# Picked keys stored in threes, and two heads' scores together: one Trainium2 core

## The reference

```python
# L0 attention, d = 4 heads of h = 64
scores = jnp.einsum('bdsh,bdth->bdst', q, k) / SCALE
weights = jax.nn.softmax(scores, axis=-1)
feats = jnp.einsum('bdst,bdth->bdsh', weights, v)
...
# L1 attention: 32 heads of 2, B = 4, S = 512
h = jnp.einsum('bsd,fd->bsf', xn, W1)
pair = jax.nn.relu(h[:, :, None, :] - h[:, None, :, :] + b1)
pair = jax.nn.relu(jnp.einsum('bijf,gf->bijg', pair, W2) + b2)
sim = jnp.einsum('bijg,og->bijo', pair, W3)[..., 0] + b3[0]
sim = sim.at[:, diag, diag].set(0.0)
k_sparse = max(1, int(S * SPARSITY))          # 51
_, top_idx = jax.lax.top_k(sim, k_sparse)
...
scores = jnp.einsum('bhid,bhjd->bhij', q, k) / math.sqrt(HEAD_DIM)
attn = jax.nn.softmax(scores + mask[:, None, :, :], axis=-1)
ao = jnp.einsum('bhij,bhjd->bhid', attn, v)
```

## Time and profile before

| what | us |
|---|---|
| three runs, median (lowest to highest) | 2091.67 (2086.42 to 2092.28) |
| the profiled execution, and its span | 2091.8, 2090.0 |
| PE, DVE, ACT, POOL busy in the span | 1664.5, 1452.1, 1260.5, 1253.6 |
| `first_attention`, first to last scores | 31.4 to 207.1 |
| `pairwise_attention`, first L1217 to end of last L1274 | 677.9 to 2028.0 |

### The profile page before, as it was taken

One profiled execution on the slowest core, in us unless ns is written; L12 is line 12 of the kernel. 1 busy time (PEld: TensorE's weight loads), 2 busy tenths in 40 slices (PEclk: granted clock), 3 DMA queues, 4 the chain that ended last, 5 costly groups with the idle time before them and its releaser, 6 DMA issues. The chain is left out here.

```text
span 2090.0 us, 34828 instructions
## 1 busy us (share of the span) xinstructions
PE 1664.5 (80%) x13143; PEld 680.4 (33%) x13143; DVE 1452.1 (69%) x2776; ACT 1260.5 (60%) x1755; POOL 1253.6 (60%) x1107
## 2 busy tenths in 40 slices
PE   6999687888205999999989889889889889984016
PEld 3444454666104333332222223223223223221014
DVE  4555542333347566998988988889989889986656
ACT  3555301332002999999879779779879779873001
POOL 0000067665562037888888888878877887887721
PEclk9999889999657999999999999999999999997556
DMA  8300133999430001111111111111111111111101
GB/s 281 126 1 1 32 102 125 323 353 324 135 90 21 1 22 50 42 43 44 41 45 42 43 45 42 44 45 44 43 44 45 44 44 44 43 43 49 46 18 41
DMA packets 98263, 157.35 MB, mean 75 GB/s; under 512 B 23088, under 2 KB 66224, under 8 KB 98096
## 3 DMA queue, kind: packets, MB, share of 16 engines
q0 software_dynamic: 40448, 95.49, 15.7%
q1 hardware_dynamic: 40240, 42.85, 6.1%
q10 hardware_dynamic: 17408, 16.78, 2.4%
HBM read 109.94 MB, written 45.09 MB: 74 GB/s over the span
## 5 line engine op out<-in xcount | busy, mean ns | idle before, releaser
L1208 POOL DMA_INDIRECT sgot<-kv_rows,sat x816 | 993.1, 1217 | 350.1 <-issue 245.1
L1376 PE MATMUL spre<-sunit,w2t 128*32 128x512 f32 x8192 | 958.3, 604 | 94.3 <-DVE sunit L1217 89.0
L1335 ACT ACTIVATE sunit<-spre,b 128x1024 f32<-128x1024 f32 x512 | 570.5, 1114 | 170.3 <-PE spre L1376 168.5
L1217 DVE TENSOR_SCALAR sunit<-hneg,hplus 128x512 f32<-128x512 f32 x1280 | 543.6, 487 | 56.2 <-PE spre L1376 53.5
L1329 ACT ACTIVATE sunit<-hneg,hplus 128x512 f32<-128x512 f32 x768 | 521.4, 713 | 0.6 <-PEq L1015 0.6
L1376 PEld LDWEIGHTS spre<-sunit,w2t 128*32 128x32 f32 x8192 | 284.5, 111 | 715.7 <-issue 513.4
L1386 PE MATMUL ssims<-sunit,bands 128*32 128x512 f32 x2048 | 274.3, 603 | 0.4 <-ACT sunit L1335 0.4
L1243 DVE TENSOR_TENSOR sgot<-sgot,q 128x3264 f32<-128x3264 f32 x16 | 56.9, 3558 | 175.7 <-DMA sgot<-kv_rows,sat 175.7
L587 POOL MEMSET ebefore<- 128x128 f32 x1 | 0.2, 205 | 223.0 <-POOLq L221 223.0
L1386 PEld LDWEIGHTS ssims<-sunit,bands 128*32 128x32 f32 x2048 | 73.1, 113 | 156.0 <-issue 153.5
L807 ACT ACTIVATE epxt<-ebank 128x512 f32<-128x512 f32 x64 | 38.2, 597 | 114.4 <-DVE eyout L776 94.2
(11 more groups left out here) (238 smaller groups left out, 1724.4 us busy)
## 6 DMA issues: line engine op xcount, KB each, us to landing
slot_rows<-blank SPq DMA_DIRECT2D x4, 4096.0 KB, 26.7
ewgu<-gate_up SPq DMA_DIRECT2D x128, 128.0 KB, 4.5
exin<-slot_rows POOLq DMA_DIRECT2D x64, 256.0 KB, 5.9
slot_out<-eyout ACTq DMA_DIRECT2D x64, 256.0 KB, 5.2
sgot<-kv_rows,sat POOLq DMA_INDIRECT x816, 2.8
x<-L_attn_x SPq DMA_DIRECT2D x4, 512.0 KB, 5.8
out<-ftmp SPq DMA_DIRECT2D x4, 512.0 KB, 3.2
slot_rows<-erows,eslot POOLq DMA_INDIRECT x64, 2.4
```

Of the source, the lines that this page charges most:

```text
L1208: pool.indirect_dma_start(out=got[:, n % 2, key, :], out_offset=None, in_=k.kv_rows[:, :], in_offset=bass.IndirectOffsetOnAxis(ap=at[:, n ...
L1217: ve.tensor_scalar(out, a, c, 0.0, ALU.add, ALU.max).then_inc(on_vector, 1)
L1335: act.activation(unit2[:, t % 2, 2 * h:2 * h + 2, :], pre[:, h, :, :], ACT.Relu, bias=b2[:, 0:1]).then_inc(hidden, 1)
L1376: mm = pe.matmul(pre[32 * g:32 * g + 32, h, c % 2, :], k.w2t[:, 32 * (g % 2):32 * (g % 2) + 32], unit1[:, t % R, 2 * c + g // 2, :], start ...
```

## The change

In `pairwise_attention` the products of a tile go to a new tensor `prod` of shape [17, 64, 3]: 51 keys are 17 groups of three, and the three keys of a group lie next to each other for each of 64 (dimension, head). `weigh_keys` reads `got` in order and writes `prod`, in steps of three numbers (12 bytes); `add_dims`, `take_peak_off` and the exp go through it in order; the reductions read runs of three; `weigh_values` reads `got`, and the weights in steps of three, and writes `prod` in steps of three, in two halves by dimension, the second of which writes over the weights. `add_dims` is two instructions too. `score` and one half of `sim` are gone, and `peak`, `total`, `inv`, `mixed` move into `blank` (all in SBUF). The search rounds stand at steps 2, 3, 5, 9, 10, 11 and 15, the pieces of the attention at steps without a round where there is one (4, 6, 7, 8, 13, 14, and 0, 1, 2 of the next tile), each between first-layer instructions. The exp is at step 9. In every fourth step one of ACT's three first-layer rows goes to VectorE.

In `first_attention` the units of a pair of heads alternate between the two heads, and in each even slot PE makes the scores of two units, from the two halves of the partitions.

```diff
+        def unit(u):
+            pair, within = divmod(u, 2 * TB)
+            q, e = divmod(within, 2)
+            return 2 * pair + e, q
...
-                if s < END:
+                if s < END and s % 2 == 0:
...
-                    if s >= 3:
-                        pe.wait_ge(exped, s - 2)
+                    if s >= 2:
+                        pe.wait_ge(exped, s - 1)
...
-                    r = HD0 * (h % 2)
-                    pe.matmul(scores[:, s % 3, :], qk[r:r + HD0, b % 2, h // 2, q * P:(q + 1) * P],
-                              qk[r:r + HD0, b % 2, 2 + h // 2, :], start=True, stop=True).then_inc(scored, 1)
+                    for e in range(2):
+                        half = slice(e * HD0, (e + 1) * HD0)
+                        pe.matmul(scores[:, (s + e) % 3, :], qk[half, b % 2, h // 2, q * P:(q + 1) * P],
+                                  qk[half, b % 2, 2 + h // 2, :], start=True, stop=True).then_inc(scored, 1)
...
-    ON_VECTOR, ON_SCALAR = ((0, 1, 2), (4, 5)), ((3,), (6, 7))
+    ON_SCALAR = 3 * (((3,), (6, 7)),) + (((3,), (7,)),)
+    ON_VECTOR = 3 * (((0, 1, 2), (4, 5)),) + (((0, 1, 2), (4, 5, 6)),)
...
-        score = sb("score", [P, KEEP, HEADS1])
-        peak, total, inv = (sb(n, [P, HEADS1]) for n in ("peak", "total", "inv"))
-        mixed = sb("mixed", [P, KW])
+        prod = sb("prod", [P, THREES, KW, 3])
+        peak, total, inv = (k.blank[:, a:a + HEADS1] for a in (192, 224, 256))
+        mixed = k.blank[:, 288:288 + KW]
...
+        def threes(n, lo, t0=0, t1=THREES, wide=HEADS1):
+            return got[:, n % 2, 3 * t0:3 * t1, lo:lo + wide].rearrange("p (t e) n -> p t e n", e=3)
+        by_key = lambda a: a.rearrange("p t h e -> p t e h")
+        by_head = lambda a: a.rearrange("p t h e -> p h t e")
+        scores = prod[:, :, 0:HEADS1, :]
...
-            ve.tensor_tensor(keys(n), keys(n), over_keys(k.q[:, n, :], KW), ALU.mult).then_inc(attend, 1)
+            ve.tensor_tensor(by_key(prod[:, :, :, :]), threes(n, 0, wide=KW), over_keys(k.q[:, n, :], KW), ALU.mult).then_inc(attend, 1)
...
-            ve.tensor_reduce(peak[:, :], by_head, AX.X, ALU.max).then_inc(attend, 1)
+            ve.tensor_reduce(peak, by_head(scores), AX.XY, ALU.max).then_inc(attend, 1)
...
+        def weigh_values(ve, n, d):
+            half = slice(d * HEADS1, (d + 1) * HEADS1)
+            if d == 0:
+                ve.wait_ge(attend, n * ATTEND + USED - 1)
+            ve.tensor_tensor(by_key(prod[:, :, half, :]), threes(n, KW + half.start), by_key(scores),
                              ALU.mult).then_inc(attend, 1)
...
-            ve.tensor_reduce(mixed[:, :], values(n).rearrange("p k n -> p n k"), AX.X, ALU.add).then_inc(attend, 1)
+            ve.tensor_reduce(mixed, by_head(prod[:, :, :, :]), AX.XY, ALU.add).then_inc(attend, 1)
...
+        ROUND_AT = (2, 3, 5, 9, 10, 11, 15)
+            values_of, keys_of, found = n - 3, n - 2, n - 1
...
+                if u == 0 and not late:
+                    weigh_values(ve, values_of, 0)
+                elif u == 0:
+                    invert(ve, values_of)
+                elif u == 1 and not late:
+                    mix_values(ve, values_of)
+                elif u == 2 and not late:
+                    normalise(ve, values_of)
...
+                if u == 4 and late:
+                    weigh_keys(ve, keys_of)
+                elif u == 6:
+                    add_dims(ve, keys_of, int(late))
+                elif u == 7 and late:
+                    find_peak(ve, keys_of)
+                elif u == 8 and late:
+                    take_peak_off(ve, keys_of)
+                elif u == 13 and late:
+                    add_up(ve, keys_of)
+                elif u == 14 and late:
+                    weigh_values(ve, keys_of, 1)
...
+                    for j in first:
+                        first_layer(ve, n * STEPS + u, j)
+                    between(ve, n, u, False)
+                    for j in second[:1]:
+                        first_layer(ve, n * STEPS + u, j)
+                    between(ve, n, u, True)
+                    for j in second[1:]:
+                        first_layer(ve, n * STEPS + u, j)
...
-                if u == 12 and n >= 2:
+                if u == 9 and n >= 2:
                     weights_of_keys(act, n - 2)
```

More of the change, by code:

```diff
@@ L375, in _ @@
                     u = s - LAG
-                    h, q = divmod(u, TB)
+                    h, q = unit(u)
                     act.wait_ge(turned, u + 1)
@@ L1190, in pairwise_attention, with rows_done @@
         block = local.enter_context(nc.Block())
+        def rows_done(split, t, h):
+            turn, part = divmod(t, len(split))
+            done = lambda steps: sum(len(rows) for halves in steps for rows in halves)
+            return turn * done(split) + done(split[:part]) + done((split[part][:h + 1],))
         def first_layer_of(t, j):
@@ L1220, in clear_diagonal @@
             q = n % TB
-            own = sim[:, n % 2, q * P:(q + 1) * P]
+            own = sims[n % 2][:, q * P:(q + 1) * P]
             ve.wait_ge(sim_out, n + 1)
@@ L1242, in weigh_keys @@
                 ve.wait_ge(gathered[n % 2][r], 16 * COUNTS[r] * (n // 2 + 1))
-            ve.tensor_tensor(keys(n), keys(n), over_keys(k.q[:, n, :], KW), ALU.mult).then_inc(attend, 1)
-        def add_dims(ve, n):
-            ve.wait_ge(attend, n * ATTEND + 1)
-            ve.tensor_tensor(score[:, :, :], keys(n)[:, :, 0:HEADS1], keys(n)[:, :, HEADS1:KW], ALU.add).then_inc(attend, 1)
+            ve.tensor_tensor(by_key(prod[:, :, :, :]), threes(n, 0, wide=KW), over_keys(k.q[:, n, :], KW), ALU.mult).then_inc(attend, 1)
@@ L1249, in find_peak, with add_dims @@
+        def add_dims(ve, n, z):
+            part = (slice(0, 8), slice(8, THREES))[z]
+            ve.wait_ge(attend, n * ATTEND + WEIGHED)
+            ve.tensor_tensor(prod[:, part, 0:HEADS1, :], prod[:, part, 0:HEADS1, :], prod[:, part, HEADS1:KW, :],
+                             ALU.add).then_inc(attend, 1)
         def find_peak(ve, n):
-            ve.wait_ge(attend, n * ATTEND + 2)
-            ve.tensor_reduce(peak[:, :], by_head, AX.X, ALU.max).then_inc(attend, 1)
+            ve.wait_ge(attend, n * ATTEND + SUMMED)
+            ve.tensor_reduce(peak, by_head(scores), AX.XY, ALU.max).then_inc(attend, 1)
@@ L1260, in add_up @@
-            ve.wait_ge(attend, n * ATTEND + 5)
-            ve.reciprocal(inv[:, :], total[:, :]).then_inc(attend, 1)
-        def weigh_values(ve, n):
-            by_dim = values(n).rearrange("p k (d h) -> p k d h", d=HD1)
-            ve.tensor_tensor(by_dim, by_dim, score[:, :, :].unsqueeze(2).broadcast_to([P, KEEP, HD1, HEADS1]),
+            ve.tensor_reduce(total, by_head(scores), AX.XY, ALU.add).then_inc(attend, 1)
+        def weigh_values(ve, n, d):
[3 more added lines that the diff above has]
+            ve.tensor_tensor(by_key(prod[:, :, half, :]), threes(n, KW + half.start), by_key(scores),
@@ L1272, in normalise @@
         def normalise(ve, n):
[L1273 removed]
+            ve.wait_ge(attend, n * ATTEND + MIXED)
             ve.tensor_tensor(k.ao[:, n, :].rearrange("p (h d) -> p d h", d=HD1),
[L1275 to L1289 removed]
+                             mixed.rearrange("p (d h) -> p d h", d=HD1),
+                             inv.unsqueeze(1).broadcast_to([P, HD1, HEADS1]), ALU.mult).then_inc(attend, 1)
@@ new lines, in pairwise_attention, with between @@
+        ROUND_AT = (2, 3, 5, 9, 10, 11, 15)
+        def between(ve, n, u, late):
+            values_of, keys_of, found = n - 3, n - 2, n - 1
+            if 0 <= values_of < TILES:
+                if u == 0 and not late:
[6 more added lines that the diff above has]
+                    normalise(ve, values_of)
@@ L1290, in between @@
             if 0 <= found < TILES:
-                if u == 4:
+                if u == ROUND_AT[0] and late:
                     clear_diagonal(ve, found)
-                for r in range(ROUNDS):
-                    if u == 5 + (3 * r) // 2:
-                        find_best(ve, found, r)
-            if 0 <= early < TILES:
-                if u == 7:
-                    weigh_keys(ve, early)
-                elif u == 9:
-                    add_dims(ve, early)
-                elif u == 10:
-                    find_peak(ve, early)
-                elif u == 12:
-                    take_peak_off(ve, early)
+                if u in ROUND_AT:
+                    r = ROUND_AT.index(u)
+                    if not late and r:
+                        drop_best(ve, found, r - 1)
+                    elif late:
+                        find_best(ve, found, r)
@@ L1351, in _ @@
                 for h in range(2):
-                    for j in ON_SCALAR[h]:
+                    for j in ON_SCALAR[t % len(ON_SCALAR)][h]:
                         first_layer_on_scalar(act, t, j)
@@ L1357, in _ @@
                     second_unit(act, t, h)
-                    for j in ON_SCALAR[h]:
```

(1 more changed line is left out.)

75 lines of the change are left out of this document (25 added, 50 removed).

## The result

| | before | after |
|---|---|---|
| median of four runs each (lowest to highest), us | 2089.05 (2084.59 to 2092.28) | 2117.07 (2112.47 to 2124.22) |
| span of the profiled execution, us | 2090.0 | 2122.5 |

The ratio is 1.0139, with a 95% interval of 1.0098 to 1.0179. The forecast was 2032 us, faster; the time is outside its range of 1970 to 2090. Two things happened: first attention gave back what was predicted, and pairwise attention lost nearly twice as much. The profiled execution is the longest of the four (2124.22 us), so the 32.5 us between the two spans are more than the 28 between the medians.

A forecast was written before the change was run, and what follows sets the result against it. Pairwise attention was taken to be bound by POOL's gathers. Terms -21, -2.5, -2.8 and -29 summed to -55 us, from 2092 to 2037, stated as 2032 for the spreading; range 1970 to 2090.

The forecast's parts named there:

- Step 3: Pairwise attention: gathers' time lost to holds falls about 1.4 us a tile, -21 us over 15 tiles (-60 to +60).
- Both value halves: Pairwise attention: the two halves of `weigh_values` hold gathers 3.2 us a tile, between 1.25 each and 3.4 for both.
- The late burst: VectorE's unpaused first-layer rows and small products behind the last reduction: gather excess 1.6 us a tile in place of 3.6.
- Spreading breaks up first-layer runs: Pairwise attention: spread-out pieces also shorten runs of first-layer instructions, taking the forecast from 2037 to 2032 us.
- Step 2: Products at a 12-byte stride: +0.35 us for `weigh_keys`, +0.3 for `weigh_values`; high end 4.0 us a tile.
- B: Rival: strided products cost the long stride's price, 4.0 us a tile, paid by POOL; 2085 or 2106 us; chance 0.14.
- Step 1: VectorE's three reductions take 2.0, 2.0 and 3.9 us, 3.5 us less a tile; hidden except once in the tail.
- Step 4: Start of pairwise attention's gathers: first gather at 757.8 instead of 760.3, so -2.5 us.
- Step 5: Tail, from the last `weigh_keys` to the end of `normalise`, 24.5 us: reductions -3.5, longer products +0.7, so -2.8 us.
- D: Rival: early rounds make VectorE wait each tile for `take_sim`, PE starves; beyond POOL's cover about 2050; with A 0.17.
- First attention: Paired scores cost PE 1.1 us a pair, spanning 145 us, not 175; -29 us (0 to -33).
- rival A: First attention: the two units' scores don't overlap on PE, giving 2061 us; chance with D together 0.17.

The follow-up runs named there:

- e4: The changed kernel with the query copied once to PSUM, where `weigh_keys` reads it; 2050.32 us, ratio 0.9818 to the kernel before.
- e9: e1's kernel plus a closing block timing gathers beside several kinds of VectorE instruction, and strided products; eight gathers beside two-SBUF-operand products took 13.9 us.
- e2: The changed kernel with the old key layout, products contiguous and in place, new order and halves kept; 2106.99 us, ratio 1.0101 to the kernel before.
- e11: The changed kernel with `add_dims`, `take_peak_off` and both `weigh_values` halves each behind a search, early rounds kept; 2106.40 us, ratio 1.0088 to the kernel before.
- e1: The kernel before with only the new first attention (pairs of scores); 2057.79 us, ratio 0.9859 to the kernel before.

## Why the prediction was wrong
- *POOL bound, VectorE's waits for keys.* Right, before and after. I am wrong, it said, if the products take over 5 us, if the scores' span doesn't shrink, or if POOL waits for VectorE. None of this came: the products took 4.5 and 2.6 us. That list lacked what did happen; the sign for it stood in the sentence before, a mean gather below 1.19 us, and it was 1.285.
- *Step 3, POOL's excess a tile.* This is the step that failed. It put 1.4 us a tile less (bounds 4 either way), 21 us in all; over 16 tiles the excess went from 219 to 274, 3.4 us a tile more, 55 us in all. Its own terms don't give its sum: -0.2 for the values, +0.1 for `add_dims`, -2.0, +0.6 and +0.6 are -0.9, so 14 us and not 21. Term by term in the steady tiles:
  - Both value halves: predicted 3.2, measured 6.2. This is the largest miss. A half holds a gather past its own end, into the rows behind it, and I had bounded it by its own length, 3.4 for both.
  - `take_peak_off`: +0.6, measured +1.1. `add_dims`: 1.2 to 1.5, measured 1.4.
  - The longer products: +0.6 in all, measured +0.8 for the keys alone.
  - The late burst: 2.0 less, measured 0.3 less beside the mix and up to 1.5 more beside runs of rows. "Spreading breaks up first-layer runs", which took the last 5 us off the forecast, had the wrong sign: the longest run of a steady tile grew from ten to eleven.
  - The 1.9 us beside `clear_diagonal` did go, which I hadn't priced.
- *The rule of the Trainium skill* ("SBUF — State Buffer", Who interferes with whom), by which a two-input product doesn't stall descriptor writing, is marked there as inferred: e4 and e9 disagree with it for two SBUF operands (1.67 against 1.25 us a gather). The same section also says that a VectorE instruction with two SBUF inputs contends with a GpSimd instruction that reads SBUF, and a gather reads its indices (`sat`) there; with that sentence, which I passed over, the traces agree, and with the one that an instruction with at most one SBUF input doesn't contend they agree for the product with its query in PSUM.
- *Step 2, the stride.* +0.35 and +0.3 us predicted, +1.0 and +1.7 measured; within the bound of 4.0 in sum. The rule on lines of the Trainium skill ("Advanced Engine Details and Errata", Memory Cachelines) names a penalty but no size; at the price that B gave it, the long stride's, it would be 2.0 us for 3264 elements. e9 has 1.0, and no more for a second side. Rival B's end came true (slower, excess above its 2.3 us a tile), its mechanism didn't: e2 with contiguous products is at 1.0101.
- *Step 1, reductions.* 2.0, 2.0, 3.9 predicted; 1.85, 1.85, 3.55 in the tail. *Step 4, start:* -2.5, measured -3.1. *Step 5, tail:* -2.8, measured 24.5 to 22.5, -2.0, as the products are longer.
- *D, the wait for `take_sim`.* Its mechanism is there: `clear_diagonal` waited 62.7 us in all for ACT, up to 9.2. It lies under POOL's bound, as D had it for steady tiles; e11 has 32.8 of it and its ratio is only 0.5% lower, with overlapping intervals.
- *First attention.* -29 predicted, -31.5 at its end; the pair's four score matmuls take 1.13 us, as two did, so rival A is out:
```profile
123.38 1.13 PE L460 MATMUL a0scores<-a0qk 64*128 64x512 f32 x4
```
The loss behind it was not foreseen: a stretch that the change doesn't touch was priced at its old clock. It was 13.5 us in the profiled execution and 4 to 7 in the five others. Over the whole kernel e1 still has 29 us of gain, so this part of the forecast stands.

Sum with the measured terms: -31.5 + 13.5 - 3.1 + 55.6 - 1.8 - 0.2 = +32.5, where -55 stood.

## What to carry to other kernels
Where gathers on POOL are the bound, read how long each gather lies beside VectorE's instructions, and price an edit by how many stretches there are in which a gather is held, and what stands right behind them, not by the products' lengths alone: a product cut in two, its halves two steps apart, made two such stretches. Beside a product with an operand in PSUM, and beside reductions, the gathers ran free; moving one operand was worth more (3.2% of this kernel) than the whole reordering cost (2.4 or 2.5%). And here all six traces with the shorter first attention, on chips like this one, had a lower clock in the routing behind it (0.50 to 0.59 where it was 0.78): give stages that a change doesn't touch a few microseconds' doubt.

## What was not expected of the hardware
- A product with two SBUF operands lets one gather in per instruction (e9, one every 1.67 us); with one operand in PSUM (e4, e9) gathers run at their free 1.25 us, and the product takes as long as before (1.68 us for 1536 elements either way).
- Rows of `tensor_scalar` back to back cost a gather 0.15 us each in e9, 0.2 to 0.3 in the kernel, but now and then hold one until the run ends (3.26 us under eleven). What decides which of the two happens stayed open; neither the run's length nor the moment of the gather's start does alone.
- A stride of 12 bytes costs VectorE 0.3 ns an element in e9, whether one operand or all have it; reductions that read runs of three took 1.85 and 3.55 us in the tail, as contiguous ones would by the estimate from the earlier trace rows.
